# Row sums of three adjacency groups in rows 0 to 10: columns of ones on TensorE in place of adds on VectorE

## The reference

```
def _L0_gnn_ref(x, adj, W):                      # adj: 8192 x 8192, float32
    A_hat = adj + jnp.eye(adj.shape[0])
    d_inv_sqrt = jnp.sum(A_hat, axis=1) ** (-0.5)
    A_norm = d_inv_sqrt[:, None] * A_hat * d_inv_sqrt[None, :]
    support = x @ W.T
    return jax.nn.relu(A_norm @ support)

x = x + _L0_gnn_ref(_layernorm(x, axis=-1), adj, W)
x = x + _L0_ffn_ref(_layernorm(x, axis=-1)[None], ...)   # attention, experts
```

## Time and profile before

| | us |
|---|---|
| median of three runs | 3520.46 |
| lowest and highest | 3517.39, 3522.1 |
| profiled execution | 3524.27 |
| its span in the profile | 3522.5 |
| TensorE busy in the span | 3085.2 |
| VectorE busy in the span | 2554.2 |
| first adjacency group landed | 10.0 |
| last degree step of the first pass begins | 867 |

### The profile page before, as it was taken

One profiled execution on the slowest core, in us unless ns is written; L12 is line 12 of the kernel. 1 busy time (PEld: TensorE's weight loads), 2 busy tenths in 40 slices (PEclk: granted clock), 3 DMA queues, 4 the chain that ended last, 5 costly groups with the idle time before them and its releaser, 6 DMA issues. The chain is left out here.

```text
span 3522.5 us, 56503 instructions
## 1 busy us (share of the span) xinstructions
PE 3085.2 (88%) x22241; PEld 1353.5 (38%) x22241; DVE 2554.2 (73%) x2736; ACT 1423.8 (40%) x2843; POOL 1728.2 (49%) x1113
## 2 busy tenths in 40 slices
PE   2678889899989987998999999999999999957992
PEld 1334434344434432433433333333333333324661
DVE  8888887675554455779878977877987898616773
ACT  0000000000000003666666666666666666745661
POOL 0000000000321113776888699877699869763665
PEclk9778999999999997999999999999999999988996
DMA  9898876678667944440000000000000000002224
GB/s 376 349 391 366 349 308 267 282 296 302 254 261 292 359 155 167 160 164 13 29 18 18 7 24 17 11 8 7 7 17 18 11 2 17 9 26 93 74 74 154
DMA packets 157501, 506.75 MB, mean 144 GB/s; under 512 B 20081, under 2 KB 66298, under 8 KB 112326
## 3 DMA queue, kind: packets, MB, share of 16 engines
q1 hardware_dynamic: 111400, 448.58, 32.9%
q10 hardware_dynamic: 33024, 31.47, 2.7%
q0 software_dynamic: 12816, 23.11, 2.0%
HBM read 426.31 MB, written 75.37 MB: 142 GB/s over the span
## 5 line engine op out<-in xcount | busy, mean ns | idle before, releaser
L1223 DVE TENSOR_REDUCE unit_max<-ps_max 128x2 f32<-128x1024 f32 (+2 forms) x1088 | 1225.9, 1171 | 297.4 <-PE ps_max L1452 254.1
L998 POOL TENSOR_TENSOR chunk_sum<-chunk_sum,probs 128x1024 f32<-128x1024 f32 x480 | 1132.3, 2359 | 287.8 <-ACT probs L1093 277.1
L1093 ACT ACTIVATE probs<-ps_ring 128x512 f32<-128x512 f32 x2112 | 1089.8, 596 | 440.2 <-PE ps_ring L1471 408.1
L566 PE MATMUL ps_gather<-ring,keep_attended 128*128 128x512 f32 x1688 | 789.8, 625 | 140.1 <-DMA ring<-in_adj 121.4
L1471 PE MATMUL ps_ring<-q_stack,keep_shared 97*128 97x512 f16 x2112 | 673.9, 385 | 27.7 <-ACT probs L1093 22.2
L1486 PE MATMUL ps_acc<-probs,keep_shared 128*32 128x256 f32 (+1 forms) x8448 | 566.8, 386 | 0.0
L566 PEld LDWEIGHTS ps_gather<-ring,keep_attended 128*128 128x128 f32 x1688 | 332.6, 202 | 541.7 <-issue 541.7
L367 DVE TENSOR_TENSOR work<-work,ring 128x2048 f32<-128x2048 f32 x195 | 446.6, 2290 | 34.5 <-DMA ring<-in_adj 30.7
L342 POOL DMA_DIRECT2D scratch_lower<-lower x13 | 7.3, 560 | 805.0 <-ACT lower L484 805.0
L1452 PE MATMUL ps_max<-k_heads,q_heads 32*128 32x512 f16 (+3 forms) x2176 | 276.0, 378 | 69.9 <-DVE unit_max L1223 48.5
L1495 PE MATMUL ps_acc<-probs,keep_ones_heads 128*32 128x256 f32 (+1 forms) x4224 | 327.9, 380 | 0.0
(11 more groups left out here) (243 smaller groups left out, 2667.5 us busy)
## 6 DMA issues: line engine op xcount, KB each, us to landing
ring<-in_adj SPq DMA_DIRECT2D x302, 1024.0 KB, 13.9
keep_shared<-in_adj SPq DMA_DIRECT2D x45, 1024.0 KB, 10.8
scratch_slots<-empty_rows SPq DMA_DIRECT2D x16, 2080.0 KB, 14.3
moe_x_rows<-scratch_slots SPq DMA_DIRECT2D x39, 260.0 KB, 2.7
moe_parts<-scratch_parts SPq DMA_DIRECT2D x32, 256.0 KB, 4.2
x_in<-in_x SPq DMA_DIRECT2D x16, 256.0 KB, 13.3
x_in<-in_x ACTq DMA_DIRECT2D x16, 256.0 KB, 7.5
work<-in_cos ACTq DMA_DIRECT2D x16, 256.0 KB, 4.1
```

Source lines behind the costliest of these rows:

```text
L566: last = nc.tensor.matmul(bank[:], support[:, s * SUB + c, :], tile_of[g, is_again][:, c * BT:(c + 1) * BT], start=(first and c == 0), sto ...
L998: steps.then(nc.gpsimd.tensor_tensor(totals, totals, weights, ALU.add))
L1093: nc.scalar.activation(probs[:, q % SLOTS, i, kv, :, lo:], halves(bank)[:, :, lo:], ACT.Exp, scale=SCALE).then_inc(ring_read, 1)
L1223: nc.vector.tensor_reduce(unit_max[:, half % 2, heads, s % 2, unit], ps_max[:, base:base + HEADS, at:at + width], AX_X, ALU.max).then_inc( ...
```

## The change

In rows t = 0 to 10 the last three of the far groups in the load order (blocks 13, 14 and 15, the list `by_rows[t]`) are not added by VectorE. TensorE sums them in a new step ("rows", t) behind support(t): for each group, four float32 matmuls, one for each sub-block of 512 columns, whose stationary operand is 128 x 32 (`first_ones`, ones in the first column, zeros in the others). Each writes its own quarter of the 128 partitions of a new PSUM tile, `ps_rows`. ScalarE copies that tile to `row_sums` (the buffer `rotated[0]`, which the first pass does not use otherwise). degrees(t) then takes, for each of its four columns, one more matmul, of `row_sums` with the column of ones.

The slots of these groups are released to SyncE by the end of rows(t) (`rows_summed`), no longer by VectorE. `ps_v`, used in the second pass, shares the new PSUM bank. GpSimd fills the constant before the first load lands.

```diff
+    ROWS_TO, TAKEN = 11, 3
...
+    by_rows = {t: [s for s in order[t] if s > t and not stays(t, s)][-TAKEN:] for t in range(ROWS_TO)}
...
-        steps_one += later[:2] + [("turn", t)] + later[2:3] + [("support", t)] + later[3:]
+        steps_one += later[:2] + [("turn", t)] + later[2:3] + [("support", t)]
+        steps_one += [("rows", t)] * (t in by_rows) + later[3:]
...
+        first_ones = sb("first_ones", [P, HD])
+        row_sums = rotated[0]
...
-                    if not was_again:
+                    if not was_again and by_products(*before):
+                        sp.wait_ge(rows_summed, rows_taken[before[0]])
+                    elif not was_again:
                         sp.wait_ge(group_summed, summed[before])
...
                 for n in range(NB):
-                    add_group(t, n)
+                    if not by_products(t, order[t][n]):
+                        add_group(t, n)
...
+                if t in by_rows:
+                    act.wait_ge(rows_summed, rows_taken[t])
+                    nc.scalar.copy(row_sums[:], ps_rows[:]).then_inc(rows_copied, 1)
...
+                if t in by_rows:
+                    pe.wait_ge(rows_copied, rows_taken[t])
                 for s in range(SUB):
...
+                    if t in by_rows:
+                        last = nc.tensor.matmul(ps_degree[:, s:s + 1], row_sums[:, s * P:(s + 1) * P], ones[:],
+                                                start=False, stop=True)
                 last.then_inc(degree_summed, 1)
+
+            def sum_rows(t):
+                if rows_taken[t] > 1:
+                    pe.wait_ge(rows_copied, rows_taken[t] - 1)
+                for n, s in enumerate(by_rows[t]):
+                    pe.wait_ge(*loaded_by[(t, s), False])
+                    for c in range(SUB):
+                        last = nc.tensor.matmul(ps_rows[c * HD:(c + 1) * HD, :], first_ones[:],
+                                                tile_of[(t, s), False][:, c * BT:(c + 1) * BT],
+                                                start=(n == 0), stop=True, skip_group_check=True)
+                last.then_inc(rows_summed, 1)
```

More of the change, by code:

```diff
@@ L194, in graph_stage @@
         ps_q, ps_q_half, ps_k, ps_k_half = ps_support, ps_gather[2], ps_gather[3], ps_degrees
-        ps_v = ps("ps_v", [P, SUB, NKV * HD])
+        ps_rows = ps("ps_rows", [P, BT])
+        ps_v = ps_rows[:, 0:SUB * NKV * HD].rearrange("p (s c) -> p s c", s=SUB)
         ring_loaded = [sem(f"ring_loaded{s}") for s in range(R)]
@@ L219, in graph_stage @@
         degree_parts = sem("degree_parts")
+        rows_summed = sem("rows_summed")
+        rows_copied = sem("rows_copied")
         degree_summed = sem("degree_summed")
@@ L263, in graph_stage @@
             loaded_by[g, is_again] = (semaphore, 16 * len(loads_of[slot]))
-        summed = {g: n + 1 for n, g in enumerate(first_reads)}
+        by_products = lambda t, s: t in by_rows and s in by_rows[t]
+        summed = {g: n + 1 for n, g in enumerate(g for g in first_reads if not by_products(*g))}
+        rows_taken = {t: n + 1 for n, t in enumerate(sorted(by_rows))}
         STACKED_BY_POOL = NB - 2
@@ L321, in _ @@
             nc.gpsimd.memset(ones[:], 1.0).then_inc(constants_ready, 1)
+            nc.gpsimd.memset(first_ones[:, 0:1], 1.0).then_inc(constants_ready, 1)
+            nc.gpsimd.memset(first_ones[:, 1:HD], 0.0).then_inc(constants_ready, 1)
             nc.gpsimd.memset(ident[:], 0.0).then_inc(constants_ready, 1)
@@ L325, in _ @@
             nc.gpsimd.memset(keep["ones_heads"][:], 1.0).then_inc(constants_ready, 1)
-            pool.wait_ge(constants_ready, 5)
+            pool.wait_ge(constants_ready, 7)
             nc.gpsimd.affine_select(out=ident[:], in_=ident[:], compare_op=ALU.not_equal, fill=1.0, base=0,
@@ L335, in _ @@
                                     channel_multiplier=-1).then_inc(constants_ready, 1)
-            pool.wait_ge(constants_ready, 8)
+            pool.wait_ge(constants_ready, 10)
             nc.gpsimd.tensor_copy(keep["ident16"][:], ident[:]).then_inc(constants_ready, 1)
-            pool.wait_ge(constants_ready, 9)
+            pool.wait_ge(constants_ready, 11)
             for t in range(len(resumed)):
@@ L528, in _ @@
                 act.wait_ge(v_ready, n + 1)
-                nc.scalar.copy(keep["v"][:, t * SUB:(t + 1) * SUB, :], ps_v[:]).then_inc(v_copied, 1)
+                nc.scalar.copy(keep["v"][:, t * SUB:(t + 1) * SUB, :], ps_v).then_inc(v_copied, 1)
                 act.wait_ge(high_ready, n + 1)
@@ L549, in _ @@
             pe.wait_ge(weights_loaded, 16 * 7)
-            pe.wait_ge(constants_ready, 9)
+            pe.wait_ge(constants_ready, 11)
             def multiply(g, is_again):
@@ L593, in sum_degrees @@
                         last = nc.tensor.matmul(ps_degree[:, s:s + 1], total[:, c * BT + s * P:c * BT + (s + 1) * P],
-                                                ones[:], start=(c == 0), stop=(c == parts - 1))
+                                                ones[:], start=(c == 0), stop=(c == parts - 1 and t not in by_rows))
+                    if t in by_rows:
+                        last = nc.tensor.matmul(ps_degree[:, s:s + 1], row_sums[:, s * P:(s + 1) * P], ones[:],
+                                                start=False, stop=True)
                 last.then_inc(degree_summed, 1)
+            def sum_rows(t):
[8 more added lines that the diff above has]
+                last.then_inc(rows_summed, 1)
             def turn_strip(n):
@@ L627, in project @@
                 last.then_inc(v_ready, 1)
-            pieces = {"degrees": sum_degrees, "turn": turn_norm, "support": find_support}
+            pieces = {"degrees": sum_degrees, "turn": turn_norm, "support": find_support, "rows": sum_rows}
             for step in steps_one:
```

## The result

The changed kernel takes 3558.0 us in the median of four runs, the kernel before 3521.3 on the same chip: ratio 1.0105, 95% interval 1.0087 to 1.0122, some 37 us slower. The prediction was 3545 in 3530 to 3566. The profiled execution's span grew by 33.8 us.

A forecast was written before the change was run, and what follows sets the result against it. It took TensorE's list and the slots it frees as the bound, not VectorE. Ones 19.6 plus degree steps 10.5, less 1.7 for row 0 and 4 for the clock, gave 24.4 us more: 3545 us, range 3530 to 3566.

The forecast's parts named there:

- The bound: First pass: TensorE frees the slots whose loads it later waits for; VectorE is in this chain only at row 0's end.
- The ones: rows(t) on TensorE: 2.8 us a step, idle time in the first four rows, on the chain in rows 4 to 10, 19.6 us.
- the fourth rival: rows(t): tiles not side by side, 3598 us; only weight loads not, 5.2 us a step, 3562; chance 0.04.
- Row 0: End of row 0: with VectorE's three adds removed, its last add ends at 50.3 instead of 52.03, a 1.7 us gain.
- The held slots: Loads blocked until rows(t) ends, rows 5 to 11: costed at nothing; as a rival starving TensorE, 3565 us, chance 0.10.
- The degree step: degrees(0) to degrees(10): four more matmuls each, 0.87 us a row and 0.9 more in degrees(0), all on the chain, 10.5 us.
- on the same clock: Sign for degree steps in rows 4 to 7: about 4.4 us each, with TensorE's clock unchanged.
- The clock: Before (3,0) and (4,0): shorter idle time saves clock loss, -4 us (0 to 7); rival, clock stays up, 3519, chance 0.10.

The follow-up runs named there:

- bursts alone: The kernel before with rows(0) to rows(3) added on TensorE, VectorE still adding all groups, sums unused, degree steps unchanged: ratio 1.0001 to the kernel before.
- no extra degree: The changed kernel without the four added matmuls in each degree step: ratio 1.0062 to the kernel before, 22 us slower.
- longer steps alone: The kernel before with only four more matmuls, by a column of zeros, in each of degrees(0) to degrees(10): ratio 1.0038, 13 us slower.
- rows 0 to 3: The kernel before with the change made only in its first four rows, t = 0 to 3: ratio 1.0033, 11.6 us slower.

## Why the prediction was right, and where it was off

**The bound: right.** Behind row 0 VectorE is not in the chain. Its adds left out bring 0.04% (0.9996), and even in the kernel in which it is 48.60 of 50 us busy its relief moves (4,0) by 0.04 us.

**The ones: right.** 2.72 us a step against 2.8, on the chain in rows 4 to 10, 7 x 2.72 = 19.0 us against 19.6. Where they stand in a wait instead, 23 us come back. The four tiles run side by side. The rule of the Trainium skill ("TensorE: Matmul & The Clock Gate", Part 3), by which a step would take the 5.2 us of the fourth rival, doesn't hold here: 2.72 us for 24 instructions are 113 ns each, and a weight load alone takes 110.

**Row 0: right.** VectorE's last add there ends at 50.7 (predicted 50.3, 52.03 before), and degrees(0) starts 1.3 us earlier against 1.7.

**The held slots: right.** The waits ahead of (t,3) in rows 6 to 10 are 6.55, 6.7, 6.9, 6.5 and 6.5 us, against the 6.63 of the earlier trace rows before. SyncE waits 167.8 us for the ones, but in rows 6 to 10 no product behind (t,3) has an idle time ahead of it, so TensorE doesn't pay for that. VectorE's waits for ring loads grow (66.8 us against 30.7) and cost nothing, as VectorE is not the bound.

**The degree step: right by length.** 4.39 us in row 6, as predicted, and 1.7 + 10 x 0.9 = 10.7 in all. That it would run "on the same clock" was wrong in rows 4 and 5, where the step takes 5.70 and 4.94 us. What happens to the clock is the next point.

**The clock: the step that failed.** I had written that I would be wrong if (4,0) came 10 us or more away from 192, and it came 10.1 later. I took 4 us off for the ones that shorten the idle time before (3,0) and (4,0). The three products (2,0), (3,0) and (4,0) take 6.39 + 6.20 + 5.05 = 17.64 us after and 5.16 + 6.29 + 6.23 = 17.68 before: no gain. (Bursts alone gain 4.1 us in row 3 of the table below, in the fastest of ten executions; the median shows nothing of it.) The ones in rows 1 to 3 run at the lower level themselves (1.93 us for 8 instructions, against 24 in 2.72 us in row 6) and another 9 us of idle time follow. And there is a loss that I did not see: the clock falls inside the degree step or right behind it. Of before, row 2, TensorE's timeline:

```profile
95.38 5.16 PE L566 MATMUL ps_gather<-ring,keep_attended 128*128 128x512 f32 x8 [21.42 <-DMA ring<-in_adj]
100.38 3.63 PE L593 MATMUL ps_degrees<-ones,work 128*128 128x1 f32 x32
105.28 8.78 PE L566 MATMUL ps_gather<-keep_shared,keep_attended 128*128 128x512 f32 x16 [1.27 <-DVE keep_attended L376]
113.89 3.60 PE L566 MATMUL ps_gather<-ring,keep_attended 128*128 128x512 f32 x8
```

From (2,0) to (2,1) pass 18.51 us here and 23.30 after. In after the step starts at 2.4 GHz, 0.95 us for 8 instructions (103.46), and ends at 1.2 GHz, 1.85 for 8 (107.28); it takes 6.1 us, and the 16 instructions of closing(1) behind it 9.87, against 8.78. Of the 4.79 us, 1.23 lie in (2,0) itself, which stays at the lower level for longer; 2.46 lie in the degree step, 0.9 of them its length; and 1.10 lie in closing(1).

The lateness of (4,0), put together from starts in the profiled executions (each line is the time from one start to the next):

```
                          before  bursts  no extra  longer   rows    after
                                  alone   degree    degrees  0 to 3
start of (2,0)             95.38   97.71   95.42    97.32    96.45   97.23
(2,0) to (2,1)             18.51   18.54   20.42    20.54    23.02   23.30
(2,1) to (3,0), loads      26.99   28.42   27.09    26.96    28.11   28.30
(3,0) to closing(2)        16.50   12.43   16.41    14.65    17.21   17.25
closing(2) to (4,0), loads 34.84   34.78   34.69    34.76    35.98   36.24
start of (4,0)            192.22  191.88  194.03   194.23   200.77  202.32
```

After against before: 1.9 us until (2,0), 4.8 in row 2, 0.8 in row 3, and 1.3 and 1.4 in the two stretches in which TensorE waits for loads. Here prediction and result go apart: near 192 was forecast, 202.3 came, and that is most of the 12.3 us by which the median's 36.7 us lie above the sum of 24.4. From (4,0) to (11,3) the delay grows by 28.8 us, of which ones and lengths are 19.0 + 8 x 0.9 = 26.2. Behind (11,3) 5.1 us come back; in the other kernels above with the old load order that part is 11 us shorter to 4 us longer than before, so I don't read a cause into it. That the time fell into the range is therefore partly luck: no term held the 10.1 us at (4,0), and the 5.1 us that come back have no known cause.

**Packets of code in the stretches of loads.** For two lines of the table, the stretches in which TensorE waits for loads, the traces show what goes with the longer times. The changed kernel's DMA queues from 100 to 150 us (packets, MB, share) have a line that the same query of before does not:

```profile
q8 instruction: 1, 0.02, 0.1%
```

It is one packet of 16 KB of instructions, at 135.2 us, and it takes 1.06 us while the adjacency loads run. There are three such stretches, from (1,0) to (2,0), from (2,1) to (3,0) and, from (3,2) on, to (4,0); with six kernels that makes 18, and nine of them hold such a packet: all three in the changed kernel and in rows 0 to 3, the first two in bursts alone, the first in no extra degree. These nine take 30.6 to 31.0, 28.1 to 28.4 and 25.7 to 25.9 us; the nine without one 29.6, 27.0 to 27.1 and 24.4 to 24.5. So a stretch can be longer with the bursts alone too, and where the packets fall goes with 3.9 of the 10.1 us: 1.2, 1.3 and 1.4. That is read from the traces; no run moved a packet by itself, and why one of 16 KB costs more than 1 us of loads that run over sixteen DMA engines is not shown.

**What stays open.** Neither the bursts alone nor the longer steps alone nor all but the longer steps make (4,0) later than the 194.6 that the unchanged rows 0 to 3 reach by themselves; both together make it 7 to 10 late, in four kernels. The stretches with code packets (3.9 us) and the added lengths (3.1 us by (4,0)) come to 7.0 of the 10.1 in the changed kernel. The rest is where in a row the clock rises and falls; what sets that, and why bursts and longer steps do it only together, was not found.

## What to carry to other kernels

A busy engine need not be the bound: look at who frees the slot whose load the other engines wait for, and at what it costs to give that one more to do. Before moving work between engines, look whether a load stands in its queue behind one that waits for the consumer; reordering loads gave 78 to 100 us here, where moving work cost 37. If work has to go to the engine on the chain, put it into a wait of that engine, not behind it (here 14 us in place of 37).

## What the hardware showed

Short bursts of work between idle times don't keep TensorE's clock up. In rows 1 to 3 of the kernels with the old load order, where three bursts lie in the idle time, most ran at the lower level (1.93 us) and one here and there at the higher (1.06 us, at 132.28 in bursts alone). After the 9 to 11 us of idle time that follow, the next product began at the lower level in every case.

In the six kernels of the table, in rows 2 to 4, the length of (t,0) foretells the degree step behind it in all 18 cases: where (t,0), begun at 1.2 GHz after the idle time, takes 5.88 us or less, so that the clock rose early in it, the degree step runs at 2.4 GHz throughout (3.5 to 3.6 us, or 4.4 to 4.5 with the added matmuls); where it takes 6.08 or more, the clock falls within the step (4.3 to 4.7, or 6.1 to 6.4 us). That was so in 10 of the 18. In six of the other eight the granted clock fell within 1.3 us behind the step's end, and the products behind paid: closing(1) takes 8.78 us before and 9.99 with the longer steps alone. Only twice, both with the bursts alone, did it stay up. So the step of one-column matmuls is where the clock goes down, in it or right behind it, and a longer step then pays twice for a part of its instructions.

One packet of 16 KB of instructions (0.9 to 1.1 us on its queue) among 1 MB loads goes with a stretch of loads that is some 1.0 to 1.5 us longer: so it was in all nine stretches that hold one, against the nine that hold none.

Matmuls whose stationary operand has 32 columns, in four different column tiles, run side by side even with all rows of the array in use: 24 float32 instructions of 512 columns take 2.72 us, 113 ns each, against 429 ns for one of full width.
